# Attention in rounds of a whole third of a head: blocks of eleven value products, four PSUM banks for the row maxima

## What is computed

```python
h = _layernorm(x, ln1_g, ln1_b)
q = (h @ wq + bq).reshape(B, S, N_HEADS, dk)      # 8 heads of 32, S = 1354
k = (h @ wk + bk).reshape(B, S, N_HEADS, dk)
v = (h @ wv + bv).reshape(B, S, N_HEADS, dk)
scores = jnp.einsum('bqhd,bkhd->bhqk', q, k) / np.sqrt(dk).astype(np.float32)
attn = jax.nn.softmax(scores, axis=-1)
ctx = jnp.einsum('bhqk,bkhd->bqhd', attn, v).reshape(B, S, D)
x = x + ctx @ wo + bo
```

## Time and profile before

| | us |
|---|---|
| median of 3 runs (1038.51 to 1040.2) | 1039.08 |
| the profiled execution | 1038.09 |
| its span on the core | 1036.1 |
| first maxima product to last value product | 120.9 to 381.3 |
| PE busy in the whole span | 826.5 (80%) |
| DVE busy | 519.1 (50%) |
| ACT busy | 383.7 (37%) |
| mean granted clock of PE, share of full speed | 0.892 |

### The profile page before, as it was taken

How to read it: one execution, slowest core, us unless ns; L and a number is a source line. 1 busy time by engine, 2 the same in 40 slices (tenths; PEclk the granted TensorE clock), 3 DMA queues, 4 the chain that set the end, 5 groups by cost and what they waited for, 6 DMA issues and landing times.

```text
span 1036.1 us, 12707 instructions
## 1 busy us (share of the span) xinstructions
PE 826.5 (80%) x3873; PEld 575.2 (56%) x3874; DVE 519.1 (50%) x1013; ACT 383.7 (37%) x787; POOL 86.4 (8%) x87
## 2 busy tenths in 40 slices
PE   4968799999999995069997259954299999999930
PEld 3856555555555343069997238733156666666630
DVE  4035677666666856468884538757022222222213
ACT  1004325565555644036664143120044444444410
POOL 2000000000000000530000300003600000000025
PEclk9998759999999998579999588985599999999975
DMA  7496802123331110135441635062201000111014
GB/s 253 146 322 263 201 23 59 39 69 73 77 68 35 28 27 0 42 115 190 169 168 53 250 171 195 28 261 105 77 26 30 30 30 30 33 35 34 25 41 130
DMA packets 54465, 102.39 MB, mean 99 GB/s; under 512 B 17978, under 2 KB 46220, under 8 KB 52764
## 3 DMA queue, kind: packets, MB, share of 16 engines
q1 hardware_dynamic: 51260, 94.16, 28.1%
q0 software_dynamic: 3168, 7.77, 2.4%
HBM read 72.16 MB, written 23.54 MB: 92 GB/s over the span
## 4 chain that ended last, share of the span: by engine, by line
PE 72%; DVE 10%; issue 6%; POOL 4%; DMA 4%; ACT 2%; SPq 1%; POOLq 0%; ACTq 0%; DVEq 0%
PE ps L1163 11%; PE ps L930 10%; PE ps L1145 9%; PE ps L910 6%; PE ps L861 5%; PE ps L922 5%; PE ps L1094 4%; PE ps L1015 3%; PE ps L1016 3%; PE ps L1017 3%; PE ps L1154 2%; DVE mx L1302 2%; PE ps L849 2%; POOL xs_d L648 1%; PE ps L1109 1%
## 5 line engine op out<-in xcount | busy, mean ns | idle before, releaser
L1302 DVE TENSOR_REDUCE mx<-ps 128x1 f32<-128x452 f32 x264 | 148.1, 622 | 70.0 <-PE ps L910 68.7
L716 ACT ACTIVATE expo<-ps 128x452 f32<-128x452 f32 x264 | 124.3, 551 | 111.6 <-PE ps L922 110.7
L930 PE MATMUL ps<-expo,v_st 128*64 128x452 f32 (+1 forms) x576 | 117.4, 529 | 0.0
L910 PE MATMUL ps<-k_st,q_st 96*128 96x452 f32 x264 | 111.6, 452 | 4.9 <-DMA k_st<-k_hi_d 4.8
L1163 PE MATMUL ps<-w_l,h 128*128 x464 | 109.1, 389 | 6.7 <-ACT h L832 4.1
L832 ACT ACT_TABLE_LOAD x29 | 37.2, 1283 | 189.3 <-PE ps L1154 189.3
L1145 PE MATMUL ps<-w_l,x1t_t 128*128 x232 | 106.0, 600 | 1.2 <-DVE x1t_t L1603 1.2
L1163 PEld LDWEIGHTS ps<-w_l,h 128*128 128x128 f32 x464 | 86.8, 192 | 24.7 <-issue 13.8
L922 PE MATMUL ps<-q_st,k_st 98*128 98x452 f32 x264 | 96.7, 387 | 2.0 <-ACT expo L716 2.0
L1608 DVE COPY h1pre<-ps 128x1024 f32<-128x1024 f32 x29 | 35.5, 1225 | 113.8 <-PE ps L1145 113.8
L910 PEld LDWEIGHTS ps<-k_st,q_st 96*128 96x128 f32 x264 | 54.5, 207 | 52.7 <-DVE mx L1302 35.7
(11 more groups left out here) (235 smaller groups left out, 1230.2 us busy)
## 6 DMA issues: line engine op xcount, KB each, us to landing
w_l<-w_l SPq DMA_DIRECT2D x8, 2053.0 KB, 8.5
w_l<-w_l SPq DMA_DIRECT2D x2, 8208.0 KB, 23.5
adj<-adj_t SPq DMA_DIRECT2D x22, 704.0 KB, 4.1
xs_d<-zeros SPq DMA_DIRECT2D x1, 3712.0 KB, 20.3
x1t<-xs_d SPq DMA_DIRECT2D x29, 128.0 KB, 2.1
ys_d<-y1t SPq DMA_DIRECT2D x29, 128.0 KB, 1.7
q_st<-q_hi_d SPq DMA_DIRECT2D x16, 176.0 KB, 3.1
k_st<-k_hi_d SPq DMA_DIRECT2D x16, 176.0 KB, 4.1
```

The lines of the kernel that those rows point to most:

```text
L716: act.activation(expo[g % 8][:, :], ps[:, 3 + g % 3, 0:QC], ACT.Exp, scale=SCALE).then_inc(s_exp, 1)
L910: pe.matmul(ps[:, i % 3, 0:KC], q_st[h % 3][0:3 * DK, (n // KB) * P:(n // KB + 1) * P], k_st[h % 3][0:3 * DK, (n % KB) * KC:(n % KB + 1) * ...
L930: return pe.matmul(ps[at:at + 2 * DK, 6 + g // T % 2, lo:hi], v_st[h % 2][:, kt, :], expo[g % 8][:, lo:hi], start=kt < 2, stop=kt == T - 1 ...
L1302: dve.tensor_reduce(mx4[:, n // KB, n % KB:n % KB + 1], ps[:, i % 3, 0:KC], AX_X, ALU.max).then_inc(s_mx, 1)
```

## The change

- The cut into 4, 4 and 3 units goes: a group is a whole third, so there are 24. PE's order for a group is now 11 scores with 11 or 12 slots of maxima between them, then 11 units of value products. A first round of scores with 8 slots stands ahead of the loop.
- The maxima have four banks, 0, 1, 2 and 7, and the context one, bank 6. Value products of a new third wait for the copy of the one before. The output product of tile 6, which uses bank 6, waits for the last copy.
- There are 20 exponential buffers. The exponential of unit g waits for the value product of unit g - 20. PE's value products wait for their exponentials one by one and no longer for the group's last.
- ACT copies third j - 1 out after the exponentials of third j.
- The second weight buffer of the experts gives its room to the exponential buffers; it moves over v, and its first load comes after all attention.
- On SP, the maxima of the next head are stored after the head's first third and no longer after its second.

```diff
-PARTS = (4, 4, 3)
+EXPOS = 20
...
-        w_l0 = [place(f"w_l0_{i}", [WCOLS]) for i in range(2)]
+        w_l0 = [place("w_l0_0", [WCOLS])]
         attn_at = cursor[0]
...
-        expo = [place(f"expo{i}", [QC]) for i in range(8)]
+        expo = [place(f"expo{i}", [QC]) for i in range(EXPOS)]
...
         cursor[0] = attn_at
+        w_l0.append(place("w_l0_1", [WCOLS]))
...
-        GROUPS = [range(third * T + sum(PARTS[:n]), third * T + sum(PARTS[:n + 1]))
-                  for third in range(H * THIRDS) for n in range(len(PARTS))]
+        GROUPS = [range(n * T, (n + 1) * T) for n in range(H * THIRDS)]
...
         FILL = TURN[0] + 7
+        MAX_BANKS = (0, 1, 2, 7)
         AHEAD = 8
...
-            return min(SLOTS, FILL + -(-SLOTS * (phase + 1) // len(GROUPS)) + min(phase + 1, AHEAD))
+            return min(SLOTS, FILL + AHEAD + -(-SLOTS * (phase + 1) // len(GROUPS)))
...
-            for e in range(2):
-                sp.dma_start(w_l0[e][:, :], a["w_l0"][e]).then_inc(s_w0[e], 16)
+            sp.dma_start(w_l0[0][:, :], a["w_l0"][0]).then_inc(s_w0[0], 16)
...
-                store_third(h, 1)
                 if h + 1 < H:
                     load_max(h + 1)
+                store_third(h, 1)
             store_third(H - 1, 2)
+            sp.wait_ge(s_av, PRIMED + H * UNITS)
+            sp.dma_start(w_l0[1][:, :], a["w_l0"][1]).then_inc(s_w0[1], 16)
...
-                if g >= 8:
-                    act.wait_ge(s_av, PRIMED + g - 7)
-                act.activation(expo[g % 8][:, :], ps[:, 3 + g % 3, 0:QC], ACT.Exp, scale=SCALE).then_inc(s_exp, 1)
+                if g >= EXPOS:
+                    act.wait_ge(s_av, PRIMED + g - EXPOS + 1)
+                act.activation(expo[g % EXPOS][:, :], ps[:, 3 + g % 3, 0:QC], ACT.Exp, scale=SCALE).then_inc(s_exp, 1)
...
-                act.activation(ctx_raw[n % 2][:, :], ps[:, 6 + n % 2, 0:QC], ACT.Identity).then_inc(s_cr, 1)
+                act.activation(ctx_raw[n % 2][:, :], ps[:, 6, 0:QC], ACT.Identity).then_inc(s_cr, 1)
...
-                if j and j % len(PARTS) == 0:
-                    copy_third(j // len(PARTS) - 1)
+                if j:
+                    copy_third(j - 1)
...
-                if i >= 3:
-                    pe.wait_ge(s_mx, i - 2)
+                if i >= 4:
+                    pe.wait_ge(s_mx, i - 3)
...
-                if first % T == 0 and first >= 2 * T:
-                    pe.wait_ge(s_cr, PRIMED + first // T - 1)
-                pe.wait_ge(s_exp, PRIMED + group[-1] + 1)
+                if first >= T:
+                    pe.wait_ge(s_cr, PRIMED + first // T)
                 for g in group:
+                    pe.wait_ge(s_exp, PRIMED + g + 1)
...
-            for g in GROUPS[0]:
-                scores(g)
-            for j, group in enumerate(GROUPS):
-                slots = list(range(slots_by(j - 1) if j else FILL, slots_by(j)))
-                for g in GROUPS[j + 1] if j + 1 < len(GROUPS) else ():
+            def next_scores(phase):
+
+                slots = list(range(slots_by(phase - 1) if phase >= 0 else FILL, slots_by(phase)))
+                for g in GROUPS[phase + 1] if phase + 1 < len(GROUPS) else ():
                     if slots:
                         fill_slot(slots.pop(0))
                     scores(g)
                 for i in slots:
                     fill_slot(i)
+
+            next_scores(-1)
+            for j, group in enumerate(GROUPS):
+                next_scores(j)
                 group_values(group)
...
+                if t == 6:
+                    pe.wait_ge(s_cr, PRIMED + H * THIRDS)
```

More of the change, by code:

```diff
@@ L899, in fill_slot @@
             def fill_slot(i):
-                if i >= 3:
-                    pe.wait_ge(s_mx, i - 2)
+                if i >= 4:
+                    pe.wait_ge(s_mx, i - 3)
                 if i in TURN:
                     pe.wait_ge(s_hl, TURN.index(i) + 1)
-                    pe.transpose(ps[0:2 * T, i % 3, 0:P], m_hl.bitcast(F32)[:, :], ident).then_inc(s_s1, 1)
+                    pe.transpose(ps[0:2 * T, MAX_BANKS[i % 4], 0:P], m_hl.bitcast(F32)[:, :], ident).then_inc(s_s1, 1)
                 else:
@@ L909, in fill_slot @@
                         pe.wait_ge(s_stack[h % 3], h // 3 * 96 + 96)
-                    pe.matmul(ps[:, i % 3, 0:KC], q_st[h % 3][0:3 * DK, (n // KB) * P:(n // KB + 1) * P],
+                    pe.matmul(ps[:, MAX_BANKS[i % 4], 0:KC], q_st[h % 3][0:3 * DK, (n // KB) * P:(n // KB + 1) * P],
                               k_st[h % 3][0:3 * DK, (n % KB) * KC:(n % KB + 1) * KC],
@@ L929, in values @@
                 at = 2 * DK * side
-                return pe.matmul(ps[at:at + 2 * DK, 6 + g // T % 2, lo:hi], v_st[h % 2][:, kt, :], expo[g % 8][:, lo:hi],
+                return pe.matmul(ps[at:at + 2 * DK, 6, lo:hi], v_st[h % 2][:, kt, :], expo[g % EXPOS][:, lo:hi],
                                  start=kt < 2, stop=kt == T - 1, skip_group_check=True)
@@ L1298, in empty_slot @@
                         dve.wait_ge(s_mload[(h - 1) % 3], (h - 1) // 3 * 16 + 16)
-                    dve.tensor_copy(m_rows[:, :], ps[0:2 * T, i % 3, 0:P]).then_inc(s_mx, 1)
+                    dve.tensor_copy(m_rows[:, :], ps[0:2 * T, MAX_BANKS[i % 4], 0:P]).then_inc(s_mx, 1)
                 else:
                     h, n = chunk_of(i)
-                    dve.tensor_reduce(mx4[:, n // KB, n % KB:n % KB + 1], ps[:, i % 3, 0:KC], AX_X, ALU.max).then_inc(s_mx, 1)
+                    dve.tensor_reduce(mx4[:, n // KB, n % KB:n % KB + 1], ps[:, MAX_BANKS[i % 4], 0:KC], AX_X, ALU.max).then_inc(s_mx, 1)
                     if n == CHUNKS - 1:
```

## The result

The changed kernel takes 1042.75 us (median of 18 runs, 1039.51 to 1049.57) against 1038.8 for the kernel before in the same comparison: a ratio of 1.0041, 95% interval 1.0025 to 1.0057. (No ratio here is the quotient of the two medians; that would be 1.0038 in this case.) It is slower by about 4 us. I had forecast 1036.8, which is 2.3 us less than before, and a range that ended at 1042.

A forecast was written before the change was run, and what follows sets the result against it. PE was taken as the bound in attention. Rounds 1 to 19 (-3.7), start (+0.3), rounds without fills (-0.5) and the stretch after the last values (+1.6) sum to -2.3 us; against 1039.1 that forecasts 1036.8, range 1030.5 to 1042.

The forecast's parts named there:

- Value blocks and switches: Thirds 1 to 19 on PE: one eleven-unit block and fewer switches save 0.74 us a third, 14 us over nineteen.
- V: PE's stretch from the start of a block's value products to the next product; 4.32 us forecast for eleven units.
- rival C: Value blocks: each unit's own wait costs 25 ns, +6.6 us over 264 units, giving 1043.4; chance 0.07.
- Waits for DVE in rounds 1 to 18: PE waits for reductions to free maxima banks and at transpositions; forecast to eat about 10 of the 14 us.
- S: PE's stretch from first score or maxima product to value products; 5.0 (11 slots), 5.36 (12), 5.95 us (with transposition).
- Rival A: Rounds' waits for DVE stay small: rounds gain 11.4 us, the sum is -10.0, giving 1029.1; chance 0.16.
- The start: Up to the end of third 0, forecast at 160.0 against 159.73: +0.3 us, between -1.0 and +1.0 by clock rise.
- Third 19: The last round with maxima slots, only six left: S of about 5.5 us.
- Thirds 20 to 23: Rounds without maxima fills, only ACT's three banks counting, and the last block: 31.8 us against 32.37, -0.5 us.
- rival B: Rounds 20 to 22: clock falls to 1.2 GHz in S, slowing value blocks; costs 6.3 us, giving 1043.1; chance 0.13.
- After the last values: Third 22's later copy delays the last third's normalization on DVE to 6.5 to 6.9 us past values: +1.6 us.
- The moved transfers: Later second weight load and the moved maxima transfer on SP: nothing speeds up and nothing queues longer.

The follow-up runs named there:

- Three banks: The changed kernel with its maxima in three PSUM banks instead of four, bank 7 unused: 1050.55 us (one run).
- shorter reductions: The changed kernel with each maxima reduction reading only the first 226 of 452 columns: 1026.29 us (one run).
- The filler: The changed kernel with one more product, read by nobody, after each score in rounds 20 to 22: 1038.43 us, ratio to before 0.998.
- the second profile: Profile from running the changed kernel once more with no edit: 1044.28 us (12 runs), ratio to before 1.0033.
- Two groups followed by small ones: The changed kernel with thirds 0 to 18 cut into 6 and 5 units, thirds 19 to 23 into 4, 4 and 3: 1032.61 us, ratio 0.9925.
- the version with two groups: The changed kernel with every third cut into groups of 6 and 5 units: 1034.59 us (6 runs), ratio to before 0.994.

## Why the prediction was wrong

**Value blocks and switches: right.** V was forecast at 4.32 and is 4.32 wherever the clock is full, so rival C, a cost for each unit's wait, falls as well.

**Waits for DVE in rounds 1 to 18: right.** S was forecast at 5.0, 5.36 and 5.95 and is 5.02, 5.34 and 5.70. The one miss is the transposition round, 0.25 too long: PE's transposition comes 4.06 us into the round, as forecast (4.05), and what follows it takes 1.64 us and not 1.90. Three banks (5.56, 5.88, 6.06) and shorter reductions (4.80, 5.00, 4.98) move S as the law says. Over thirds 1 to 18 the forecast was 175.6 us; it is 174.2. Rival A, that the waits stay small, is refuted: they cost 7.7 us in thirds 1 to 18. I called all of this DVE's banks; over half of it lies in the rounds with a transposition.

**The start: inside the doubt that I gave it.** The clock rose at about 148 us, before the 150.4 that I took, and third 0 ends at 159.13, not 160.0. That is no finer than the scatter: with whole rounds and four banks for the maxima it ended between 158.93 and 160.41 in four profiles.

**Third 19: wrong.** I gave its S 5.5 us, counting only PE's pace behind the transposition. It is 6.72. ACT has nothing to do while PE waits for the maxima and starts its exponentials again at 337.90; of the six scores behind the transposition three go at once and three then wait for a bank, 0.44 apart. The filler, with that block at full clock, has 6.45. This is 1 us of the miss, a term left out.

```profile
337.39 0.27 PE L907 MATMUL ps<-const,m_hl 128*22 128x128 f32 x1 [1.74 <-DVE m_hl L1320]
...
337.90 1.86 ACT L718 ACTIVATE expo<-ps 128x452 f32<-128x452 f32 x4 [1.55 <-PE ps L924]
```

**Thirds 20 to 23: the step that failed.** I forecast 31.8 us, a term of -0.5 that took the full clock for granted, and named the other side as rival B, with a chance of 0.13: a clock that falls in S. Rival B is what happened, and the term came out at +3.7. With the filler the same rounds take 32.57, so the forecast without a drop was off by 0.8 at most, and some of that may be the filler's own work: the one S of such a round that stayed at full clock throughout and had no filler, in the run with three banks, is 4.65 long, with 4.62 forecast. The drop costs at least 36.04 - 32.57 = 3.5 us there and 1.3 in third 19's block. I had argued that pauses below 1 us between blocks of 4.3 us of dense work would not bring the clock down, and that the trace of before has no drop between 160 and 381. That trace had no S longer than 1.6 us at ACT's pace, so it could not say. Its own row of a cold PE that stays cold while DVE holds it to one product in 0.54 us was the nearest evidence, and I read it as speaking of the rise alone. The rival's mechanism was right; I priced it as one and a half blocks at half speed throughout, where it is four blocks each losing 1.0 to 1.3 us, and 1.2 to 1.7 in the second profile. That its sum of 1043.1 lies close to the median of 1042.75 is luck: it has 6.3 us for the clock, where the profiles show about 5 and the rest came from elsewhere. Without the drop the forecast holds: the filler, whose profile has no drop at all, is 2 us below before (1038.43 against 1040.49), with 2.3 forecast.

The Trainium skill, "TensorE: Matmul & The Clock Gate", A second HAM failure mode, tells of short idle times between groups of products, in a kernel that cycles through PSUM banks, that made the clock oscillate. The traces agree in rounds 20 to 22, where PE waits for ACT's three banks between single products and the granted clock falls (0.51 and 0.64 in the rows above), and with the filler's products between the scores it stays at 1.00. They do not agree in rounds 1 to 18, where PE also waits for banks and the clock stays at 1.00.

**After the last values: right.** The last normalization begins 7.0 us after the end of values (388.74 against 381.72), with +6.5 to +6.9 forecast and 5.1 before. Two groups followed by small ones, which copy third 22 earlier again, have 5.4 (378.64 against 373.23).

**The moved transfers: right** for the weight load, as the run with the late load alone shows. The new place of the maxima's store on SP was not run by itself.

The end of values, forecast at 160.0 + 185.5 + 31.8 = 377.3, is 377.94 with the filler and 381.72 without. Of the miss in attention the clock is nearly all; what else was off, the start, the transpositions, third 19 and the tail's 0.8, about cancels. What is left of the median's 4 us I can only bound: the first profiled run is 2.0 us above that of before, the second 6.2, and what parts these two lies between the end of values and the first gather. That stretch takes 187.5 and 188.0 us in the two profiles with the attention of before, 189.1 and 192.9 in the two of the changed kernel and 189.0 with the filler. The later normalization, 1.9 us, covers the 189.1 and not the 192.9. Whether the change makes the clock of that stretch worse or the runs differ by themselves stays open.

## What to carry to other kernels

A schedule in larger blocks must be checked where its filling work runs out: the same rounds that gained 5 us while PE had maxima to interleave lost it all once PE was held to ACT's pace for a whole S of 4.9 us. The clock took most of that, a longer S in third 19 and a later last copy the rest. Cut the blocks smaller there, or give PE something to do. And when producer and consumer alternate in blocks, count how far the consumer falls behind, and how many banks that needs: of the 12 us that fewer switches were worth here, waits for DVE took 7.7, while blocks half as long lost almost nothing to them and kept half of the switches' gain.

## What I had not expected of the hardware

In round 22 the granted clock fell while PE issued scores 0.44 us apart, having waited 0.28 us for ACT ahead of the first of them, and so it did in rounds 20 and 21. It fell in all three of these rounds in three profiles and in two of them in a fourth. In the version with two groups the S stretches of 2.0 and 2.4 us at the same pace, between blocks of 2.0 and 2.4, did not bring it down in the one profile taken. And 33 products that nobody reads made the kernel faster (1044.28 to 1038.43 us, intervals apart), since they kept the clock up for the value blocks behind them.
